# Layer norm sums taken on ScalarE in place of VectorE's statistics, in a fused attention and mixture-of-experts kernel

## The reference

```python
x = x + attention(ln_c(x))      # ln_c: mean and variance over the 128 channels, eps 1e-6
t = to_tokens(x)                # 1024 tokens of 128 channels for each image
t = t + moe(ln_t(t))            # ln_t: mean and variance over the 128 channels, eps 1e-5
x = from_tokens(t)
```

## Time and profile before

| | us |
|---|---|
| median of three runs | 2466.99 (2466.51 to 2470.71) |
| the profiled execution | 2465.24 |
| span of its trace | 2463.4 |
| attention part, batches 0 to 15 | 65.3 to 1741 of the span |
| TensorE, VectorE, ScalarE, GpSimd busy | 2135.1, 1888.8, 1472.6, 1039.5 |

### The profile page before, as it was taken

One profiled execution on the slowest core, in us unless ns is written; L12 is line 12 of the kernel. 1 busy time (PEld: TensorE's weight loads), 2 busy tenths in 40 slices (PEclk: granted clock), 3 DMA queues, 4 the chain that ended last, 5 costly groups with the idle time before them and its releaser, 6 DMA issues. The chain is left out here.

```text
span 2463.4 us, 49403 instructions
## 1 busy us (share of the span) xinstructions
PE 2135.1 (87%) x14610; PEld 1168.7 (47%) x14610; DVE 1888.8 (77%) x4599; ACT 1472.6 (60%) x2881; POOL 1039.5 (42%) x1649
## 2 busy tenths in 40 slices
PE   6999999999999999999999999998379999999953
PEld 3333333333333333333333333333178998998952
DVE  6899999999989998999989989896245455555544
ACT  1777777777777677777777767677134444444410
POOL 2204434444443454434454443443544444444420
PEclk9999999999999999999999999999589999999975
DMA  4222313233232332313233132230622222222249
GB/s 116 53 46 52 70 35 63 53 67 65 40 66 48 62 60 52 69 36 65 51 66 72 34 65 51 52 65 16 187 62 62 62 62 62 64 62 62 63 138 289
DMA packets 134679, 170.39 MB, mean 69 GB/s; under 512 B 31118, under 2 KB 101140, under 8 KB 134450
## 3 DMA queue, kind: packets, MB, share of 16 engines
q1 hardware_dynamic: 117618, 134.24, 25.4%
q0 software_dynamic: 16896, 34.12, 3.9%
HBM read 64.86 MB, written 48.86 MB: 46 GB/s over the span
## 5 line engine op out<-in xcount | busy, mean ns | idle before, releaser
L858 DVE TENSOR_REDUCE sb_m_red<-banks 128x1 f32<-128x512 f32 x2048 | 1325.4, 678 | 150.8 <-PE banks L1279 149.3
L714 ACT ACTIVATE sb_arena_a<-banks 128x512 f32<-128x512 f32 x2048 | 1115.0, 599 | 438.9 <-PE banks L1303 415.5
L1279 PE MATMUL banks<-sb_arena_b 62*128 62x512 f32 x2048 | 813.5, 466 | 105.3 <-DVE sb_m_red L858 93.2
L1303 PE MATMUL banks<-sb_arena_b 64*128 64x512 f32 x2048 | 805.2, 462 | 7.1 <-ACT sb_arena_a L714 7.1
L1279 PEld LDWEIGHTS banks<-sb_arena_b 62*128 62x128 f32 x2048 | 346.1, 187 | 769.1 <-DVE sb_m_red L858 658.9
L1320 PE MATMUL banks<-sb_arena_a,sb_arena_d 128*32 128x512 f32 x4096 | 549.0, 608 | 6.5 <-ACT sb_arena_a L714 0.7
L697 POOL DMA_INDIRECT expert_out<-sb_arena_d x272 | 267.7, 984 | 312.5 <-DVE sb_arena_d L1182 271.5
L653 POOL DMA_INDIRECT sorted_rows<-sb_rows,sb_place x256 | 251.2, 981 | 341.8 <-PE banks L1303 312.7
L1303 PEld LDWEIGHTS banks<-sb_arena_b 64*128 64x128 f32 x2048 | 337.1, 185 | 28.6 <-ACT sb_arena_a L714 28.1
L1448 PE MATMUL banks<-sb_arena_d,sb_arena_c 128*128 128x128 f32 x2176 | 291.5, 277 | 46.3 <-issue 44.3
L834 ACT ACTIVATE sb_arena_c<-banks 128x512 f32<-128x512 f32 x272 | 162.4, 597 | 226.0 <-PE banks L1448 226.0
(11 more groups left out here) (144 smaller groups left out, 1634.9 us busy)
## 6 DMA issues: line engine op xcount, KB each, us to landing
sb_arena_b<-sb_arena_c SPq DMA_DIRECT2D x768, 64.0 KB, 2.3
sb_arena_d<-sorted_rows SPq DMA_DIRECT2D x272, 66.0 KB, 1.8
sb_arena_a<-expert_out SPq DMA_DIRECT2D x32, 512.0 KB, 5.5
sb_x_in<-in_x_dram SPq DMA_DIRECT2D x16, 512.0 KB, 3.8
sb_res<-in_x_dram SPq DMA_DIRECT2D x16, 512.0 KB, 3.5
sb_x_all<-sb_res SPq DMA_DIRECT2D x16, 512.0 KB, 3.1
out_dram<-sb_arena_a SPq DMA_DIRECT2D x16, 512.0 KB, 3.8
expert_out<-sb_arena_d POOLq DMA_INDIRECT x272, 2.2
```

What stands on the lines that cost most here:

```text
L714: nc.scalar.activation(probs[:, u % PRING, :], ps_score[:, u % RING, :], ACT.Exp, scale=SCALE).then_inc(exp_done, 1)
L858: nc.vector.tensor_reduce(out=m_red[:, s % 2, at:at + 1], in_=ps_max[:, m % SLOTS % RING, :], axis=AX.X, op=ALU.max).then_inc(max_taken, 1)
L1279: nc.tensor.matmul(ps_max[:, m % SLOTS % RING, :], qs[rows_of, g, l, half * HALF + t * P:half * HALF + (t + 1) * P], ks[rows_of, g, l, kh ...
L1303: nc.tensor.matmul(ps_score[:, u % RING, :], ks[rows_of, g, l, i * P:(i + 1) * P], qs[rows_of, g, l, half * HALF:(half + 1) * HALF], start ...
```

## The change

VectorE's statistics and aggregates go. ScalarE copies each block of 128 columns by itself, with the sum of the block as a second output (`accum_out`) into `neg_mean`. GpSimd multiplies the eight sums by -1/128 (`ln_means`). ScalarE then takes the square of each block with the negative mean as bias, with the sum of the squares as a second output into `ln_var`; the squares themselves go to `v_st`, which is free then, and are not read. GpSimd's `ln_factors` has one instruction less and takes the sums of squares times 1/128. The token transposes move from units 20 and 22 to 15 and 19, and the waits on `misc` count blocks instead of halves.

```diff
+            def ln_means(b, which, copied, done):
+                wait(gp, copied, TB * (b + 1))
+                nc.gpsimd.tensor_scalar(neg_mean[:, which, :], neg_mean[:, which, :], -1.0 / C, 0.0,
+                                        ALU.mult, ALU.add).then_inc(done, 1)
             def ln_factors(b, which, eps, stats_done, done):
-                wait_apart(gp, gp_passed, stats_done, 16 * (b + 1))
-                nc.gpsimd.tensor_scalar(ln_var[:, which, :], mean_var[:, which, :, 1], 1.0, eps,
+                wait(gp, stats_done, TB * (b + 1))
+                nc.gpsimd.tensor_scalar(ln_var[:, which, :], ln_var[:, which, :], 1.0 / C, eps,
                                         ALU.mult, ALU.add).then_inc(done, 1)
-                nc.gpsimd.tensor_scalar(neg_mean[:, which, :], mean_var[:, which, :, 0], -1.0, 0.0,
-                                        ALU.mult, ALU.add).then_inc(done, 1)
...
# GpSimd, batch(b, first, last)
-                for n in rest[1:5]:
+                for n in rest[1:3]:
+                    scatter(b - 2, n, at + 4 * (n - 8) + 1)
+                if not last:
+                    ln_means(b + 1, 0, xt_copied, ln1_mean)
+                for n in rest[3:5]:
                     scatter(b - 2, n, at + 4 * (n - 8) + 1)
                 if not last:
                     normalise_x(b + 1)
+                if not first:
+                    ln_means(b - 1, 1, tok_copied, ln2_mean)
...
# ScalarE
+            def copy_xt(b, j):
+                wait(act, xt_psum, 2 * b + j // 4 + 1)
                 wait(act, v_psum, 2 * b)
+                nc.scalar.activation(xt[:, j, :], misc[:, j % 4 * P:(j % 4 + 1) * P], ACT.Copy,
+                                     accum_out=neg_mean[:, 0, j:j + 1]).then_inc(xt_copied, 1)
+            def square(b, which, j):
+                src, means, done = (xt, ln1_mean, ln1_stats) if which == 0 else (tok, ln2_mean, ln2_stats)
+                if j == 0:
+                    wait(act, means, b + 1)
...
+                nc.scalar.activation(v_st[:, j, :, :].rearrange("p h d -> p (h d)"), src[:, j, :], ACT.Square, bias=neg_mean[:, which, j:j + 1],
+                                     accum_out=ln_var[:, which, j:j + 1]).then_inc(done, 1)
...
-                        if u == 2:
-                            copy_xt(b + 1, 0)
-                        if u == 6:
-                            copy_xt(b + 1, 1)
+                        if 2 <= u < 10:
+                            copy_xt(b + 1, u - 2)
+                        if 12 <= u < 16:
+                            square(b + 1, 0, 2 * (u - 12))
+                            square(b + 1, 0, 2 * (u - 12) + 1)
...
-                        if u == 21:
-                            copy_tokens(b - 1, 0)
-                        if u == 23:
-                            copy_tokens(b - 1, 1)
+                        if u in (16, 17, 20, 21):
+                            j = 2 * (16, 17, 20, 21).index(u)
+                            copy_tokens(b - 1, j)
+                            copy_tokens(b - 1, j + 1)
+                        if 28 <= u < 32:
+                            square(b - 1, 1, 2 * (u - 28))
+                            square(b - 1, 1, 2 * (u - 28) + 1)
...
# VectorE, batch(b, first, last)
-                        if 8 <= u < 16:
-                            norm_stats(b + 1, 0, xt_copied, ln1_stats, u - 8)
-                        if u == 17:
-                            norm_means(b + 1, 0, ln1_stats)
...
-                        if 24 <= u < 32:
-                            norm_stats(b - 1, 1, tok_copied, ln2_stats, u - 24)
-                        if u == 32:
-                            norm_means(b - 1, 1, ln2_stats)
...
# TensorE
             def transpose_x(b, half):
-                misc_free(xt_copied, 2 * b + half + 1)
+                misc_free(xt_copied, TB * b + 4 * half + 4)
...
             def transpose_tokens(b, half):
-                misc_free(tok_copied, 2 * b + half + 1)
+                misc_free(tok_copied, TB * b + 4 * half + 4)
...
-                        if u == 20:
+                        if u == 15:
                             transpose_tokens(b - 1, 0)
-                        if u == 22:
+                        if u == 19:
                             transpose_tokens(b - 1, 1)
```

More of the change, by code:

```diff
@@ L233, in metaformer @@
         xt_copied = sem("xt_copied")
+        ln1_mean = sem("ln1_mean")
         ln1_stats = sem("ln1_stats")
@@ L260, in metaformer @@
         tok_copied = sem("tok_copied")
+        ln2_mean = sem("ln2_mean")
         ln2_stats = sem("ln2_stats")
@@ L657, in _ @@
             gp.wait_ge(weights_in, WEIGHTS)
+            ln_means(0, 0, xt_copied, ln1_mean)
             normalise_x(0)
@@ L737, in copy_v @@
                 wait(act, v_placed, 2 * b)
+                wait(act, ln1_stats, TB * (b + 1))
+                wait(act, ln2_stats, TB * (b - 1))
                 nc.scalar.activation(v_st[:, 4 * half:4 * half + 4, :, :].rearrange("p j h d -> p j (h d)"),
@@ L746, in copy_m, with copy_tokens @@
                 nc.scalar.activation(m_row[0:MROWS, :], misc[0:MROWS, :], ACT.Copy).then_inc(m_copied, 1)
-            def copy_tokens(b, half):
-                wait(act, tt_psum, 2 * b + half + 1)
+            def copy_tokens(b, j):
+                wait(act, tt_psum, 2 * b + j // 4 + 1)
                 wait(act, rows_normed, TB * b)
-                nc.scalar.activation(tok[:, 4 * half:4 * half + 4, :],
-                                     misc[:, :].rearrange("p (j c) -> p j c", j=4), ACT.Copy).then_inc(tok_copied, 1)
+                nc.scalar.activation(tok[:, j, :], misc[:, j % 4 * P:(j % 4 + 1) * P], ACT.Copy,
+                                     accum_out=neg_mean[:, 1, j:j + 1]).then_inc(tok_copied, 1)
             def gate_exponentials(b):
@@ L767, in copy_counts @@
                 nc.scalar.activation(counts[:, :], misc[:, 0:TB * 3 * E + 3 * E], ACT.Copy).then_inc(cs_taken, 1)
-            copy_xt(0, 0)
-            copy_xt(0, 1)
+            for j in range(TB):
+                copy_xt(0, j)
+            for j in range(TB):
+                square(0, 0, j)
             for i in range(4):
@@ L814, in _ @@
             batch(B - 1, False, True)
-            copy_tokens(B - 1, 0)
-            copy_tokens(B - 1, 1)
+            for j in range(TB):
+                copy_tokens(B - 1, j)
+            for j in range(TB):
+                square(B - 1, 1, j)
             gate_exponentials(B - 1)
@@ L901, in divide @@
                                         o_n[:, half, :, :].rearrange("p n d -> p (n d)")).then_inc(norm_steps, 1)
[L903 to L908, removed]
-                wait_apart(dve, dve_passed, done, 16 * b + TB)
-                for j in range(TB):
-                    nc.vector.bn_aggr(mean_var[:, which, j, :], stats[:, which, j:j + 1, :]).then_inc(done, 1)
             def add_residual(b, half):
@@ L936, in choose @@
                 wait(dve, lg_psum, b + 1)
-                wait(dve, ln2_scale, 3 * (b + 1))
+                wait(dve, ln2_scale, 2 * (b + 1))
                 nc.vector.tensor_tensor(out=gat[:, :, :], in0=misc[:, 0:TB * E].rearrange("p (j e) -> p j e", j=TB),
@@ L1024, in _ @@
             nc.vector.memset(stacks_f[32:SIDE, 1, :, :, :], 1.0).then_inc(key_rows, 1)
-            for j in range(TB):
-                norm_stats(0, 0, xt_copied, ln1_stats, j)
-            norm_means(0, 0, ln1_stats)
             dve.wait_ge(setup, SETUP)
@@ L1107, in _ @@
             add_residual(B - 1, 1)
-            for j in range(TB):
-                norm_stats(B - 1, 1, tok_copied, ln2_stats, j)
-            norm_means(B - 1, 1, ln2_stats)
             choose(B - 1)
```

17 lines of the change are left out of this document (8 added, 9 removed).

## The result

The changed kernel takes 2554.99 us (median of four runs, 2542.5 to 2559.87) against 2466.75 us (2463.28 to 2470.71) for the kernel before on the same chip: a ratio of 1.0344 [1.0326, 1.0363], 88 us slower. The prediction said 2502 us with a range of 2458 to 2527: the direction was right, the size was not.

What follows compares the result with a forecast made beforehand. VectorE was taken to lead in units 3 to 22, elsewhere its loop with TensorE, clock no term; 14 batches x 2.25 us, batches 0 and 15 together 0, 4.5 us one-off: +36 us, 2502 us, range 2458 to 2527.

Steps and rivals of the forecast that it cites:

- Step 1: Statistics leaving VectorE: 2.07 us per norm; first norm's worth up to 2.07 us a batch, second's up to 0.3.
- Step 2: ScalarE's 128-column copies with a sum, eight per norm: 0.26 us each, bounds 0.17 and 0.34.
- Step 3: ScalarE's squares with a sum: 0.30 us each, between 0.21 and 0.38; 7.0 us more per batch with the copies.
- Step 4: New TensorE wait at unit 5, second x transposes behind copies: 2.05 us later, project_out(0) 0.95 us late.
- Step 5: New wait at unit 17, token copies behind exponentials and eight squares of units 12 to 15: project_out(1) 3.6 us late.
- Step 6: Units 17 to 24: the 0.97 us wait goes, TensorE needs 6.3 us from project_out(1), batch 2.1 us late at unit 24.
- Step 7: Squares in units 28 to 31 put 2.4 us on ScalarE: 0.15 us late, 0 to 0.4.
- The one-off: Longer norm chains at the kernel's start, 2.5 us, and end, 2.0 us: 4.5 us together.
- A: VectorE's lead decides: new waits fall into time TensorE waits anyway, first norm's 2.07 us gained; 2440 us, chance 0.15.
- B: No change: the saving comes out in part, 0.3 us per batch, just paying the start and end cost; 2467 us, chance 0.08.
- C: Accumulator output empties ScalarE's pipe: copies 0.45 us, squares 0.48, 4.7 us per batch; 2540 us, chance 0.09.
- D: Square needs another function table: 16 loads of 1.28 us per batch, 20 us; 2770 us, chance 0.02.

Runs made afterwards that it cites:

- vector_late: Kernel before, both norms on VectorE, with project_out(1) and residual at unit 19, token transposes at 15 and 27, store of x behind the maxima's load; 2455.98 us, 0.9946.
- norm2_store: Changed kernel, first norm back on VectorE, project_out(1) and residual at unit 19, token transposes at 15 and 27, store of x behind the maxima's load; 2473.49 us, 1.0019.
- norm1_slack: Changed kernel, second norm back on VectorE; first norm's second x transposes at unit 8, later copies at 9 and 10, squares one a unit in 12 to 19; 2458.68 us, 0.9958.
- norm1_only: Changed kernel with only the first norm on ScalarE; second norm back on VectorE with token transposes at units 20 and 22; 2481.04 us, 1.0045.
- squares_late: Changed kernel with the first norm's eight squares moved from units 12 to 15 to units 18, 19, 22 and 23; 2560.72 us, 1.0364.
- move_only: Kernel before with only the token transposes moved to units 15 and 19, whole copies at 17 and 21, both norms on VectorE; 2477.4 us, 1.0037.
- norm2_only: Changed kernel with only the second norm on ScalarE, token transposes at units 15 and 19; first norm back on VectorE with whole copies; 2519.56 us, 1.0212.
- turn_back: Changed kernel with token transposes back at units 20 and 22, four token copies each in units 21 and 23, both norms on ScalarE; 2528.93 us, 1.025.

## Why the prediction was wrong in size

- **Step 1, VectorE's 2.07 us per norm**: right in kind. In the middle batches VectorE's busy time fell by 48 us, 3.4 per batch, and its idle time rose from 9.2 to 17.6 us per batch, as the stops would have it. The second norm's share does not pay for its sums on ScalarE (vector_late against norm2_store). The first's nets at most 0.6 us where TensorE isn't stopped (norm1_slack), and its places may have part in that.
- **Step 2, copies**: 0.25 us, forecast 0.26.
- **Step 3, squares**: 0.38 us against 0.30. That is the upper bound, though not for its reason: the sum costs 0.09 us there and not 0.17, and the bias the rest. Eight stand before the stop at unit 17, 0.6 us in all, but exponential 12 came earlier than in the walk (10.85 us behind exponential 0 in place of 11.4), so project_out(1) was 3.75 us late against 3.6.
- **Step 4, unit 5**: the stop 1.99 us against 2.05, the loss at project_out(0) 0.69 against 0.95. By itself (norm1_only) the first norm then loses only 0.3 us per batch at full clock, so the forecast was on the high side here.
- **Step 5, unit 17**: stop and size right, its cause only half, so that the size is in part luck. squares_late and move_only show that the round trip score unit, exponential, copy, projection makes it, and that the squares only add: without them the stop is 2.0 us in place of 2.57, where the forecast gave them 2.4 us of the chain.
- **Step 6 is the step that failed**, and with it the sentence that the clock is no term here. "From project_out(1) TensorE needs ... 6.3 us" was worked out with durations at full clock, and at full clock it holds (6.26 us in norm2_only); behind a stop of 2.6 to 3.1 us it needed 7.8. The missing term is 1.5 us in each of 14 batches, 21 us, and as much again behind unit 5 in batches 2 to 6 (7 us) and once more in batch 3 (1.4 us). Units 36 to 64 of batches 1, 4 and 5 add 3.7 us, and the 4.2 us that the kernel before lost in such units go: 29 us of clock in all. The sentence was a misreading already of the earlier trace rows, whose digits do not show those 4.2 us. Undoing the move (turn_back) leaves some 70% of the loss, some of it at the new stop of unit 24 and more of it behind unit 5, where half clock then came in 11 batches.
- **Step 7, squares 28 to 31**: 0.5 us behind unit 24 against 0.15 (bound 0.4), 5 us over 14 batches; which part of it is the squares' own price was not separated.
- **Batches 0 and 15, "together 0"**: +3.5 and +5.0. In both a stop is followed by half clock (units 5 to 8 of batch 0 take 5.15 us at 0.68, units 17 to 20 of batch 15 8.20 us at 0.58). The one-off was 3.2 us at the start and 3.0 at the end against 2.5 and 2.0.
- **The sum** itself is 1 us off: 2465.24 + 36 + 1.75 is 2503 us, not 2502.

The last step of the last norm, whose shift of 83.8 us against the earlier trace rows is 80.8 us of start and batches and 3 us of its own chain:

```profile
1830.58 0.20 POOL L529 TENSOR_SCALAR sb_ln_var<-sb_ln_var 128x8 f32<-128x8 f32 x1 [3.30 <-ACT sb_v_st L744]
```

Added up: the 14 middle batches gave 37.6 us more than forecast (29.2 of clock, 7.4 of stop and squares, 1.0 not assigned), batches 0 and 15 8.5, the rest 4.8, and 36 + 50.9 is the 86.9 us measured. About 3 us of these lie behind the last norm, where both kernels do the same, and stay unexplained.

Of the rivals, A and B fell with the two stops; C was wrong in kind, since the accumulator's own instruction moves the next by 0.09 us and not by 0.27, though its 2540 us lies nearest to the result, by chance; D fell with the one table load.

Open: why one stop is followed by half clock and its twin in another batch is not (unit 5 in batches 2 to 6 and not in 7 to 14; move_only in 2 of 14), and what lowers the clock in units 36 to 64, where no stop stands just ahead. So a stop is neither always followed by half clock nor the only thing that is. No run here varies the stop by itself. That the lower clock costs the 1.5 us is shown by batches of one kernel with the same steps and the same stop; that the stop brings it on is an inference from how often it follows: units 5 to 8 have the full clock in every batch of the middle where the stop is not there (before, norm1_slack).

## What to carry to other kernels

When a step moves ahead, follow the round trip: a wait placed in the very unit whose score feeds the engine that must answer costs the whole trip, a stop of 1.5 to 2 us here even with one plain copy as the answer; with three units of room the loss of the first norm became a gain. Price a stop of TensorE of some 2 us twice, once for itself and once, as a chance, for the stretch behind it at half clock. And don't call the clock "no term" from a page of nines: read it in windows of a few units, before and after. And for each step moved, list the in-order queues of all engines that it passes: SyncE's store and GpSimd's mean each made a stop here, worth some 23 and 14 us.

## What the runs showed of the hardware

- A sum as second output is an instruction of its own on ScalarE: rows of 214 and 233 ns in the mean, 0.09 us in the packed pace.
- A `[128,1]` bias from a tensor makes the ACTIVATE row of 128 columns 91 to 105 ns longer (401 and 415 against 310 ns).
- Behind a stop TensorE can run at 1.2 GHz for a stretch: the projection 1.80 us in place of 1.09, a pair 0.73 in place of 0.43, a weigh 1.53 in place of 1.00, some 1.4 to 1.5 us in all. In the profiled executions it came behind each of the 14 stops of 2.6 to 3.1 us before project_out(1) of the changed kernel and behind its 2.0 us in batch 15; behind 2.0 us in 12 of 15 batches of norm2_only (unit 17) and in 6 of 15 of the changed kernel (unit 5); behind 1.46 us in 2 of 15 of move_only.
- It also came with no stop just ahead: in units 36 to 64 of 4 of the 14 middle batches before (1.0 us each), and of 8 in norm2_store (1.0 to 2.7 us each). The mean clock of the 40 slices doesn't show either; windows of a few units do.
